# Two PSUM banks per signal in a graph kernel's gather by matmul

## The reference

```python
def nnconv(x, src, dst, edge_attr, ew, eb, rw, rb):      # three layers of it
    W = (edge_attr @ ew + eb).reshape(E, 16, 16)         # a 16x16 matrix per edge
    msg = einsum('ei,eio->eo', x[src], W)
    return segment_sum(msg, dst) + x @ rw + rb
...
h = relu(layernorm(x))
x = x + (three nnconv, batch norm and relu between them, then a linear layer)
h = relu(layernorm(x))
msg = h[src] * edge_weight1                              # the last stage
x = x + segment_max(msg, dst) @ W.T + b
```

## Time and profile before

| what | value |
|---|---|
| median of 3 runs | 14553.09 us (14543.45 to 14564.69) |
| the profiled execution's own time | 14536.82 us |
| its span in the trace | 14534.8 us |
| mean granted TensorE clock | 0.847 of full speed |
| busy share of the span | TensorE 73%, weight load 65%, GpSimd 52%, ScalarE 49%, VectorE 48% |

### The profile page before, as it was taken

One profiled execution on the slowest core, in us unless ns is written; L12 is line 12 of the kernel. 1 busy time (PEld: TensorE's weight loads), 2 busy tenths in 40 slices (PEclk: granted clock), 3 DMA queues, 4 the chain that ended last, 5 costly groups with the idle time before them and its releaser, 6 DMA issues.

```text
span 14534.8 us, 163770 instructions
## 1 busy us (share of the span) xinstructions
PE 10630.9 (73%) x51268; PEld 9511.0 (65%) x51268; DVE 7036.5 (48%) x11477; ACT 7049.5 (49%) x6857; POOL 7620.8 (52%) x7727
## 2 busy tenths in 40 slices
PE   4777777777477777777747777877774777777774
PEld 3666666666367666666636666766663777777774
DVE  5555555555455555555545555555552333333332
ACT  2455555455245455455425545554543555555553
POOL 5555555555445555555545555555555555555555
PEclk9888888888788888888878888888886888888887
DMA  3222222222222222222222222222221111111111
GB/s 83 64 65 63 66 64 66 63 66 67 55 61 67 63 67 64 64 65 65 64 53 66 65 66 63 68 66 62 66 64 22 27 29 28 28 28 28 28 28 20
DMA packets 371031, 801.95 MB, mean 55 GB/s; under 512 B 149635, under 2 KB 210139, under 8 KB 370719
## 3 DMA queue, kind: packets, MB, share of 16 engines
q0 software_dynamic: 247136, 425.71, 14.1%
q1 hardware_dynamic: 123839, 375.54, 8.1%
HBM read 669.76 MB, written 130.92 MB: 55 GB/s over the span
## 4 chain that ended last, share of the span: by engine, by line
PE 59%; another core or an unknown queue 19%; issue 11%; DVE 6%; ACT 3%; POOL 1%; DMA 0%; DVEq 0%; ACTq 0%; SPq 0%; POOLq 0%
PE pY L749 54%; PE pY L771 3%; ACT apart L610 2%; DVE msg L975 2%; DVE xe L892 1%; DVE gathered L279 1%; POOL gathered L555 1%; ACT hot_key L616 1%; PE pT L761 1%; PE pY L472 1%; PE pT L771 0%; DVE rows L1004 0%; ACT xeT L825 0%; DVEq L243 0%
## 5 line engine op out<-in xcount | busy, mean ns | idle before, releaser
L749 PE MATMUL pY<-part,hot_key 128*128 128x400 f32 x45384 | 9893.0, 377 | 1754.6 <-issue 1026.2
L749 PEld LDWEIGHTS pY<-part,hot_key 128*128 128x128 f32 x45384 | 9081.4, 209 | 2510.4 <-issue 1558.1
L555 POOL DMA_INDIRECT gathered<-conv_table,idx x5487 | 5439.4, 991 | 5013.5 <-DVE idx L1020 3339.5
L892 DVE TENSOR_REDUCE xe<-pY 128x16 f32<-128x400 f32 x5673 | 3131.3, 569 | 5790.5 <-PE pY L749 2729.9
L610 ACT ACTIVATE apart<-key_pair,zone_lane 128x1408 f16<-128x1408 f16 (+1 forms) x1984 | 2899.3, 1508 | 2840.3 <-remote 1815.9
L616 ACT ACTIVATE hot_key<-apart,hot_line 128x1408 fp32r<-128x1408 f16 (+1 forms) x1984 | 3086.0, 1603 | 20.9
L555 POOL DMA_INDIRECT gathered<-max_table,idx x1736 | 1689.1, 973 | 1583.0 <-DVE idx L1020 1062.3
L825 ACT COPY xeT<-pT 96x128 f32<-96x128 f32 x744 | 194.4, 261 | 3640.1 <-remote 1739.4
L975 DVE TENSOR_REDUCE msg<-gathered 128x240 f32<-128x2160 f32 x744 | 1558.8, 2095 | 0.2
L771 PE MATMUL pY<-edge_w,xeT 32*128 32x288 f32 x2976 | 639.7, 510 | 866.6 <-ACT xeT L825 598.3
L279 DVE TENSOR_TENSOR gathered<-pY,pe_attr 128x288 f32<-128x288 f32 x1488 | 608.2, 450 | 988.8 <-remote 717.6
(11 more groups left out here) (137 smaller groups left out, 1546.4 us busy)
## 6 DMA issues: line engine op xcount, KB each, us to landing
key_pair<-key_rows SPq DMA_DIRECT2D x248, 672.0 KB
scanned<-run_pair SPq DMA_DIRECT2D x248, 416.0 KB
gathered<-conv_table,idx POOLq DMA_INDIRECT x5487
attr_pair<-in_attr SPq DMA_DIRECT2D x186, 208.0 KB
gathered<-max_table,idx POOLq DMA_INDIRECT x1736
key_pair<-key_rows SPq DMA_DIRECT2D x248, 78.0 KB
conv_table<-gathered SPq DMA_DIRECT2D x36, 360.0 KB, 2.2
conv_table<-rows SPq DMA_DIRECT2D x24, 360.0 KB, 2.3
```

Of the source, the lines that this page charges most:

```text
L555: e.indirect_dma_start(out=G[s][:, t, 0:width], out_offset=None, in_=table[:, :], in_offset=bass.IndirectOffsetOnAxis(ap=idx[s][:, t:t + 1 ...
L749: ins = e.matmul(pG[bank], hot_key[s][:, z, at:at + P], part[:, z * NEAR:(z + 1) * NEAR, :], start=(z == 0 and k == 0), stop=(z == ZONES - ...
L892: e.tensor_reduce(xe[s][:, at:at + D], pG[j % BANKS].rearrange("p (r d) -> p d r", d=D), AX.X, ALU.max).then_inc(s_pick.sem, 1)
```

## The change

The four single banks become two buffers of two banks. The columns of a chunk become six units of two columns (in a chunk of 11 columns the last unit has one). TensorE fills both banks of a buffer, 16 matmuls, and signals once. VectorE picks both columns in one reduction over 800 numbers and signals once. A unit waits for the pick of the unit before the last. TensorE keeps two units ahead of its loop instead of four columns. The first transpose comes after unit 3 (column 7), the first product after unit 4 (column 9). In `body` the picks become: conv: unit 1 ahead of the sum over the near edges; indices; second `lot_product`; unit 2; sum over the far edges; `first_row`; unit 3; scan; unit 4; first `lot_product` of c1; unit 5; unit 0 of c2. Last stage: unit 1; indices; product of the picked rows; `first_row`; scan; units 2 to 5; unit 0 of c2.

```diff
-BANKS = 4
-HEAD = 4
+UNITS, AHEAD = 6, 2
+BUFFERS = 2
...
-        pG = [b[:, 0:NEAR * D] for b in (pY[0][:, 2, :], pY[1][:, 0, :], pY[1][:, 1, :], pY[1][:, 2, :])]
+        pG = [banks[:, 2 + 2 * b:4 + 2 * b, 0:NEAR * D] for b in range(BUFFERS)]
...
-                gate(e, "pe", s_pick, picked(c) + (b_pick + j - since_bank(c, j) + 1))
-                for z in range(ZONES):
-                    for k, part in enumerate(parts):
-                        ins = e.matmul(pG[bank], hot_key[s][:, z, at:at + P], part[:, z * NEAR:(z + 1) * NEAR, :],
-                                       start=(z == 0 and k == 0), stop=(z == ZONES - 1 and k == 1))
+                gate(e, "pe", s_pick, unit(c, u + (b_pick - BUFFERS + 1)))
+                for k, j in enumerate(columns(c, u)):
+                    at = (TP_KEYS - far_of(c) + j) * P
+                    for z in range(ZONES):
+                        for n, part in enumerate(parts):
+                            ins = e.matmul(pG[u % BUFFERS][:, k, :], hot_key[s][:, z, at:at + P],
+                                           part[:, z * NEAR:(z + 1) * NEAR, :],
+                                           start=(z == 0 and n == 0), stop=(z == ZONES - 1 and n == 1))
                 ins.then_inc(s_gath.sem, 1)
...
             def pe_body(e, c1, c2):
-                for j in range(HEAD, HEAD + 5):
-                    pe_step(e, c1, j)
+                pe_unit(e, c1, 2)
+                pe_unit(e, c1, 3)
                 pe_turn(e, c1, 0)
-                for j in range(HEAD + 5, HEAD + 7):
-                    pe_step(e, c1, j)
+                pe_unit(e, c1, 4)
                 pe_product(e, c1, 0)
-                for j in range(HEAD + 7, far_of(c1)):
-                    pe_step(e, c1, j)
+                pe_unit(e, c1, 5)
                 if c2 is not None:
                     pe_hots(e, c2)
-                    for j in range(2):
-                        pe_step(e, c2, j)
+                    pe_unit(e, c2, 0)
                 pe_turn(e, c1, 1)
                 if c2 is not None:
-                    for j in range(2, HEAD):
-                        pe_step(e, c2, j)
+                    pe_unit(e, c2, 1)
                 pe_product(e, c1, 1)
...
-                e.tensor_reduce(xe[s][:, at:at + D], pG[j % BANKS].rearrange("p (r d) -> p d r", d=D),
+                e.tensor_reduce(xe[s][:, js[0] * D:(js[-1] + 1) * D].rearrange("p (k d) -> p k d", d=D),
+                                pG[u % BUFFERS][:, 0:len(js), :].rearrange("p k (r d) -> p k d r", d=D),
                                 AX.X, ALU.max).then_inc(s_pick.sem, 1)
...
-                    next_picks(2)
+                    next_picks(1)
                     need(m_g)
                     pool_columns_read()
-                    next_picks(3, 4)
...
-                    next_picks(5)
...
-                    next_picks(2)
+                    next_picks(1)
                     need(m_g)
                     m_tg = total(0, near)
-                    next_picks(3)
...
-                    next_picks(4)
                     lot_product(e, c, 1)
-                    next_picks(5)
+                    next_picks(2)
...
                 m_f = first_row()
-                next_picks(6)
+                if not is_max:
+                    next_picks(3)
...
-                next_picks(7, 8, 9)
+                if is_max:
+                    next_picks(2, 3)
+                next_picks(4)
                 if not is_max and c1 is not None:
                     lot_product(e, c1, 0)
-                next_picks(*range(10, TP_KEYS))
-                head_picks(0, 1)
+                next_picks(5)
+                head_picks(0)
```

More of the change, by code:

```diff
@@ L56 @@
 assert CHUNKS % (2 * SLOTS) == 0 and CHUNKS <= P and LANES * NB == N and DIGITS == 3 and NEAR <= 2 * ZONES * ZONES
-assert all(len(p) == TILES for lots in PIECES.values() for p in lots) and TH == PAIR * TILES and LOT + PAIR * ROW <= 512 and TP_KEYS * D <= 2 * LOT and min(sum(TP_CONV, ())) >= HEAD + 7 and PE_EDGES <= NB * D
+assert all(len(p) == TILES for lots in PIECES.values() for p in lots) and TH == PAIR * TILES and LOT + PAIR * ROW <= 512 and TP_KEYS * D <= 2 * LOT and all(2 * UNITS - 2 < tp <= 2 * UNITS for tp in sum(TP_CONV + TP_MAX, ())) and TH == UNITS and PE_EDGES <= NB * D
 assert W0 * W1 * W2 == EPAD and LOOKS * LOOK == NB and W0 <= P and GB * (W1 + 1) <= 512
@@ L375, in build @@
         credits("pe", "tensor", s_tr + s_mm + [s_prod])
-        credits("dve", "vector", [s_pick] * BANKS)
-        s_pick.n = BANKS
+        credits("dve", "vector", [s_pick] * BUFFERS)
+        s_pick.n = BUFFERS
         credits("dve", "vector", [s_multiplied] * 2)
@@ L690, in far_of, with unit, columns @@
                 return tp[c[1]][c[2]]
-            def picked(c):
-                k, q, s = c
-                return k * sum(sum(tp, ())) + sum(sum(tp[0:q], ())) + sum(tp[q][0:s])
+            def unit(c, u):
+                return number(c) * UNITS + u
+            def columns(c, u):
+                return range(2 * u, min(2 * u + 2, far_of(c)))
             pair = SLOTS * T * attr_width
@@ L755, in pe_turn @@
                     return
-                a, b = LOTS[far_of(c)][half]
-                gate(e, "pe", s_pick, picked(c) + (b + b_pick))
+                gate(e, "pe", s_pick, unit(c, (half + 1) * (UNITS // 2) + b_pick))
                 gate(e, "pe", s_multiplied, number(c) * 2 + (half + b_mul))
@@ L804, in pe @@
                 pe_hots(e, first)
-                for j in range(HEAD):
-                    pe_step(e, first, j)
+                for u in range(AHEAD):
+                    pe_unit(e, first, u)
                 pe_body(e, first, (0, 0, 1))
@@ L865, in act_body @@
                 else:
-                    gate(e, "act", s_gath, picked(c1) + (far_of(c1) + b_gath))
+                    gate(e, "act", s_gath, unit(c1, UNITS + b_gath))
                     hots_begin(e, keyed, turn(c3), c3[2], b_abs, far_of(c3),
@@ L885, in edges, with pick @@
             on("scalar")(act)
-            def pick(e, c, j):
+            def pick(e, c, u):
                 s = c[2]
-                gate(e, "dve", s_gath, picked(c) + (b_gath + j + 1))
-                at = j * D
-                e.tensor_reduce(xe[s][:, at:at + D], pG[j % BANKS].rearrange("p (r d) -> p d r", d=D),
+                gate(e, "dve", s_gath, unit(c, u + (b_gath + 1)))
+                js = columns(c, u)
+                e.tensor_reduce(xe[s][:, js[0] * D:(js[-1] + 1) * D].rearrange("p (k d) -> p k d", d=D),
+                                pG[u % BUFFERS][:, 0:len(js), :].rearrange("p k (r d) -> p k d r", d=D),
                                 AX.X, ALU.max).then_inc(s_pick.sem, 1)
@@ L925, in need, with next_picks, head_picks @@
                     gate(e, "dve", s_step, n * MARKS + (base[0] + k))
-                def next_picks(*js):
-                    for j in js:
-                        if c1 is not None and j < far_of(c1):
-                            pick(e, c1, j)
-                def head_picks(*js):
-                    for j in js:
+                def next_picks(*units):
+                    for u in units:
+                        if c1 is not None:
+                            pick(e, c1, u)
+                def head_picks(*units):
+                    for u in units:
                         if c2 is not None:
-                            pick(e, c2, j)
+                            pick(e, c2, u)
                 def pool_columns_read():
@@ L1028, in vec @@
                 indices(e, (0, 0, 1))
-                for j in range(far_of(first)):
-                    pick(e, first, j)
-                    if j == 9 and not is_max:
+                for u in range(UNITS):
+                    pick(e, first, u)
+                    if u == 4 and not is_max:
                         lot_product(e, first, 0)
-                for j in range(2):
-                    pick(e, (0, 0, 1), j)
+                pick(e, (0, 0, 1), 0)
                 base[0] = s_step.n
@@ L1053, in edges @@
             for cc in (s_gath, s_pick):
-                bump(cc, rounds * sum(sum(tp, ())))
+                bump(cc, CHUNKS * UNITS)
             if not is_max:
```

14 lines of the change are left out of this document (4 added, 10 removed).

## The result

The changed kernel took 15706.18 us (median of 4 runs, 15677.71 to 15713.42), the kernel before 14553.17 us beside it (14543.45 to 14564.69): ratio 1.0793, 95% interval 1.0757 to 1.0829. I had said 14,815 us, at most 15,120. The sign was right, and the size was 4.4 times too small: +1153 us instead of +262.

A forecast was written before the change was run, and what follows sets the result against it. Each chunk was taken as bound by its gather train, the release when it lands, then VectorE's path to the next indices. 149 + 112 = 261 us on 14536.8 gave 14,798, stated as 14,815 us (+1.8%), range 14,270 to 15,120.

The forecast's parts named there:

- Price of a pair: VectorE's pick of two columns, one reduction over 800 numbers, takes 0.98 us; the saving was counted as nothing.
- Last stage: Indices now need column 3 too: +0.3 us and +2.1 us in two alternating kinds of chunk, together 149 us.
- the release: Moment a train of gathers has landed and VectorE sees columns filled late in it, about 20 us behind the train's start.
- my worse case: Last stage, first kind of chunk: unit 4 not seen as early as 8.6 us, indices at 30.0 us, +2.2 us.
- Conv layers: Later sum and unit 1 cost +0.9 us each, earlier product gains 0.6: +1.2 us a round, 112 us over 93 rounds.
- signals are what is held back one by one: Trains hold back single signals, not columns, so fewer signals shorten the path to the indices: 1054 us, 13,500 us; chance 0.07.
- The rival of the clock: Two buffers let TensorE stop longer in each train and return at 1.2 GHz: 15,120 us or more; chance 0.10.
- Fewer signals: 2697 fewer TensorE matmul signals would give 71 us by the skill's 26.3 ns each; nothing was taken for it.
- VectorE's work on the path: Pairs' saving (-190 us) lies wholly on the path and the earlier product brings its best (-130 us): 14,300 us; chance 0.20.
- nothing: Time stays within 30 us, as the train and its landing, 20 of 27 us, are untouched; chance 0.12.

The follow-up runs named there:

- order_alone_again: Kernel before with single banks, picks and signals kept, but the change's order for TensorE and VectorE: 15531.36 us, 1.0688 on a first-kind chip.
- column3_behind_indices: Kernel before with the pick of column 3 moved from ahead of the indices to behind them in the conv layers: 15371.73 us, 1.0588.
- the mirror: Kernel before with column 4's pick ahead of the indices, 1.0000; changed kernel with unit 2's pick ahead of them, 1.0085; conv layers, both second-kind chip.
- signals_per_column: Changed kernel with TensorE signalling each column again and VectorE waiting for the second column's signal before picking the pair: 1.0100 on a second-kind chip.
- pairs_conv_only: Changed code in the conv layers, last stage as in the kernel before: 1.0102 on a second-kind chip.

## Why the prediction was wrong

- *Price of a pair*: 0.98 us predicted, 986 ns measured for the 2697 picks of 800 numbers. Right, and beside the point.
- *Last stage*: +149 us predicted, +205 measured, inside the bounds. Unit 4 is seen 17 to 18 us behind the first gather in two kinds of chunk and 11 to 12 in the other two (medians), not at 8.6 as I had thought likelier; unit 5 and the rest follow at the release (20.0), as in my worse case. GpSimd's wait for indices is 1318.0 / 124 = 10.6 us, where I had said 9.8.
- *Conv layers*: +112 us predicted with a bound of 372, +952 measured. This is the step that failed. The sum wrote "3.4 us either way if both columns are there", and took what comes through a train as given ("Columns that TensorE has filled late in a train are seen by VectorE only when the train has landed" was the only rule). The traces of the first kind give, for the four kinds of chunk of the second conv layer (medians, us behind the first gather of a train):

```
                     columns 2, 3 filled        columns 2, 3 picked       next indices
                     before      changed        before      changed       before  changed
indices first, A     8.5, 9.9    8.2, 9.6       14.9, 21.9  21.4          22.4    24.9
indices first, B     12.3, 13.8  22.3, 24.4     21.6, 24.4  24.5          24.9    27.9
indices first, C     13.8, 15.2  23.8, 26.0     22.8, 25.6  26.0          26.0    29.5
behind the far sum   19.0, 21.0  25.7, 28.2     24.5, 27.1  28.3          31.8    35.6
```

  In B and C both columns were filled inside the train before, and now they are not: their buffer comes free with the pick of unit 5, at 18.5 and 20.0 us, so the near sum, which needs 2.4 us and used to start behind column 2, starts some 3 us later. In A both are filled as early as before, but VectorE no longer sees column 2 alone and early; the sum falls behind the release in full, where I had taken its 2.4 us at a little over a third, +0.9, in one chunk of the four. The last kind loses 3.8, where I had said 0.9. Over a round the indices come 10.3 us later on average in this layer (93 x 10.3 = 958, against the 952), where I had said 1.2. What the sum lacked, as I read it, is a term for the work between the write of the indices and the start of the hold-back, which decides how much TensorE can fill in the train. There the change puts more: pick 7 goes ahead of the scan, which begins at 4.1 instead of 3.7 us, and TensorE's columns 8 and 9 come behind a transpose. I even booked the earlier product as a gain of 0.6 us in one chunk of four. order_alone_again shows that the order makes 836 of the 952 us (in it the indices of these four come at 24.9, 27.9, 28.8 and 34.3). That it does so by pushing signals past the start of the hold-back follows from the delays by position and from column3_behind_indices, but the mirror that would confirm it met no such chip, and neither did TensorE's order and VectorE's order by themselves. GpSimd's wait for indices is 4552.8 / 372 = 12.2 us a chunk, where I had said 9.3.
- *The rival "signals are what is held back one by one"* (13,500 us): signals do arrive singly, 2.1 us apart in the chunk shown, but one signal more for each pair changes nothing: with and without it the changed kernel takes the same time.
- *The rival of the clock*: the gather matmuls take 9988.2 us and, in the row of before below, 9893.0: 95 us at most, part of it beside waits.

```profile
L749 PE MATMUL pY<-part,hot_key 128*128 128x400 f32 x45384 | 9893.0, 377 | 1754.6 <-issue 1026.2 <-DVE xe L892 698.2 <-DVE part L1068 16.4
```

  The rule on loss by idling between groups that the Trainium skill names ("TensorE: Matmul & The Clock Gate", A second HAM failure mode: psum-queue depth-cycling) does not decide here. The mean granted clock fell from 0.847 to 0.83, and what that can have cost lies within the 95 us.
- *Fewer signals*: the Trainium skill ("TensorE: Matmul & The Clock Gate", The cost: per-tile semaphore tail) states the 26.3 ns for each signal of matmuls packed as tiles; by it 2697 signals would be 71 us as an estimate, 0.7% of 10,000. No run here shows it: signals_per_column, with 2697 signals more than the changed kernel, lies at 1.0100 and that at 1.0090 (another set), and pairs_conv_only, which differs from it in the signals and in the last stage, lies at 1.0102 in the same set. Taking nothing for it was right.
- *VectorE's work on the path* (faster, 0.20) and *nothing* (0.12): neither; the pairs shorten VectorE's busy time (7036.5 to 6843.9 us), and no run on either kind of chip became faster by it.

Open stays by what way the trains hold TensorE's signals back (its matmuls stand still there too: 1026.2 us of "issue" ahead of them in the row above, under 10 us on the second kind), why they do so on some chips and not on others, and whether column 4 ahead of the indices would make the kernel before faster on the first kind.

## What to carry to other kernels

Where a producer's signals are late for a stretch of each cycle, price what the consumer has still to do when the stretch begins, not only what it does when the stretch is over: here half a microsecond moved past the trigger of that stretch cost 2.2 us a chunk (828 / 372). Where other work must wait for such signals anyway, keep ahead of the instruction that starts the stretch what feeds other engines (argued from these runs; the kernel that would prove it met no chip of the first kind). Do not close the pause between two such stretches either: where it went, signals were held through both. And before a "remote" wait is made the base of a forecast, run the old kernel on another chip.

## What the runs showed of the hardware

The same kernel took 14,553 and 14,522 us in two sets of runs and 9,976 to 9,999 us on four other chips, with gathers issued every 1.25 us on both kinds; its mean granted clock was 0.847 on the one kind and 0.966 on the other, and its gather matmuls were busy for 9893.0 and 8608.1 us. The larger difference in the traces is the arrival of TensorE's signals: on the first kind 57% of the 2380 picks that ended an idle time of VectorE began more than 1 us behind their matmuls, on the second none of 1405 did. Signals of VectorE and ScalarE were not late on either. The late ones belong to trains of gathers: without a pause between two trains they were held through both (90 of 90), with one they were not (0 of 1036). A change measured on one kind can be worth 7.9% there and 0.9% on the other.
